# The order of SyncE's loads and stores ahead of the experts, in an attention layer with a mixture of experts

## The reference

```
xn = layernorm(x)
q, k, v = xn @ Wq.T, xn @ Wk.T, xn @ Wv.T      # 16 heads of 32; q and k get a rotary embedding
attn = softmax(causal(q @ k.T / sqrt(32))) @ v
gate_logits = xn @ gate_w.T                     # 8 experts
w = softmax(the two largest logits of a token)
y_all = xn @ expert_w.T + expert_b
out = x + attn @ Wo.T + sum over the two experts of w * y_all
```

## Time and profile before

| | |
|---|---|
| median of 3 runs | 1002.33 us (998.8 to 1003.36) |
| the profiled execution's own time | 999.5 us |
| its span, first to last instruction | 997.7 us |
| PE busy | 929.4 us (93%) |
| DVE busy | 742.8 us (74%) |
| POOL busy | 556.1 us (56%) |
| ACT busy | 435.7 us (44%) |
| granted TensorE clock, mean | 0.987 of full speed |
| 1 MB transfers, median from issue to landing | `x_in` 13.2, `w_in` 9.7, `xT_rows` 12.7, `w_rows` 7.9 us |

### The profile page before, as it was taken

The page is one execution under the profiler, slowest core; times in us unless marked ns, Lnnn a source line. Parts: engine busy times, 40 slices in busy tenths (PEclk is TensorE's granted clock), DMA queues, the critical chain, the costliest instruction groups (busy, mean ns, idle before and its releaser), DMA issues.

```text
span 997.7 us, 18754 instructions
## 1 busy us (share of the span) xinstructions
PE 929.4 (93%) x6589; PEld 447.2 (45%) x6589; DVE 742.8 (74%) x1327; ACT 435.7 (44%) x711; POOL 556.1 (56%) x553
## 2 busy tenths in 40 slices
PE   2899988989999999979999999989999999999887
PEld 1344444434444544435555555534444444444333
DVE  7988987887889899924444444477788888788865
ACT  5367866766766443331112111224434444334442
POOL 1545576674666556653333333247877888777641
PEclk9999999999999999999999999999999999999999
DMA  6366588698686353485555555454555564555431
GB/s 240 114 215 228 144 275 307 196 316 295 191 269 259 118 198 100 161 315 181 172 177 178 171 172 176 157 206 148 187 175 174 186 192 139 159 187 173 151 108 54
DMA packets 107963, 188.63 MB, mean 189 GB/s; under 512 B 11872, under 2 KB 65248, under 8 KB 102624
## 3 DMA queue, kind: packets, MB, share of 16 engines
q1 hardware_dynamic: 97072, 152.03, 44.2%
q0 software_dynamic: 10800, 35.40, 12.7%
HBM read 117.13 MB, written 70.25 MB: 188 GB/s over the span
## 4 chain that ended last, share of the span: by engine, by line
PE 67%; DVE 11%; POOL 9%; DMA 6%; ACT 3%; issue 2%; SPq 1%; DVEq 0%; ACTq 0%; POOLq 0%
PE psum L941 18%; PE psum L1026 10%; PE psum L1035 6%; PE psum L1050 6%; PE psum L989 6%; PE psum L976 5%; PE psum L958 5%; PE psum L992 5%; PE psum L918 4%; DMA x_in<-x 3%; DVE top L1476 3%; POOL gT L574 2%; PE psum L960 2%; POOL k_hl L583 1%; POOL pT L587 1%
## 5 line engine op out<-in xcount | busy, mean ns | idle before, releaser
L754 ACT ACTIVATE pT<-psum,factors 128x512 f32<-128x512 f32 (+1 forms) x352 | 219.5, 640 | 250.7 <-PE psum L976 241.3
L1476 DVE TENSOR_REDUCE top<-psum 128x1 f32<-128x384 f32 (+3 forms) x352 | 210.2, 634 | 22.7 <-PE psum L960 21.9
L1026 PE MATMUL psum<-xT,w_att 128*128 128x512 f16 x768 | 196.4, 381 | 6.6 <-DVE xT L1427 4.7
L941 PE MATMUL psum<-w_exp,x_gT 128*128 x852 | 197.7, 382 | 1.5 <-issue 1.5
L603 POOL DMA_INDIRECT x_g<-xn_rows,tok_of x71 | 67.4, 949 | 145.2 <-PE psum L918 137.2
L958 PE MATMUL psum<-k_stack,q_stack 96*128 96x384 f16 (+3 forms) x512 | 128.5, 304 | 17.4 <-DVE top L1476 16.5
L976 PE MATMUL psum<-q_stack,k_stack 98*128 98x256 f16 (+3 forms) x512 | 128.4, 304 | 5.8 <-ACT pT L754 4.5
L1432 DVE TENSOR_TENSOR x_gT<-psum,x_gT 128x512 f16<-128x512 f32 x71 | 49.0, 691 | 108.8 <-ACT x_gT L778 108.8
L941 PEld LDWEIGHTS psum<-w_exp,x_gT 128*128 128x128 f16 x852 | 84.0, 99 | 88.1 <-issue 4.5
L778 ACT ACTIVATE x_gT<-psum 128x512 f16<-128x512 f32 x71 | 42.3, 598 | 174.0 <-PE psum L918 174.0
L587 POOL TENSOR_SCALAR_AFFINE_SELECT pT<-pT 128x512 f32<-128x512 f32 x128 | 95.3, 754 | 18.4 <-ACT pT L754 18.2
(11 more groups left out here) (175 smaller groups left out, 1278.8 us busy)
## 6 DMA issues: line engine op xcount, KB each, us to landing
y_rows<-y_sb SPq DMA_DIRECT2D x71, 256.0 KB, 2.1
w_in<-w_all SPq DMA_DIRECT2D x12, 1024.0 KB, 9.7
q_stack<-qk_rows SPq DMA_DIRECT2D x96, 128.0 KB, 2.6
k_stack<-qk_rows SPq DMA_DIRECT2D x96, 128.0 KB, 2.6
x_in<-x SPq DMA_DIRECT2D x8, 1024.0 KB, 13.2
qk_rows<-q_hl SPq DMA_DIRECT2D x32, 256.0 KB, 2.1
qk_rows<-k_hl SPq DMA_DIRECT2D x32, 256.0 KB, 2.3
xn_rows<-x_in SPq DMA_DIRECT2D x8, 1024.0 KB, 4.8
```

What stands on the lines that cost most here:

```text
L754: act.activation(p_of(j, h, heads), banks[BANK_T + (NT_ * n + k) % 2][:, 0:W], ACT.Exp, scale=factors[:, 0:1]).then_inc(exp_done, 1)
L941: now = pe.matmul(banks[s % 4], x_gT[s % 4][:, xp * C + c, :], w_exp[:, bass.ds(e, 1), wp, c, :].rearrange("p e d -> p (e d)"), start=n == ...
L1026: now = pe.matmul(bank, w_att[:, what, wp, c, g * P:(g + 1) * P], xT[b % 2][:, xp * C + c, :], start=at_pass == 0, stop=at_pass == 3 * C - 1)
L1476: return dve.tensor_reduce(out=top[:, h:h + heads, i], in_=banks[BANK_S + k % 2][:, 0:heads * W].rearrange("p (h t) -> p h t", h=heads), a ...
```

## The change

Within a step's group of large transfers, the load of the next batch of x comes first, then the store of `gT`, and then the store of a pair and the load of the next matrix. What each waits for is the same as before, and no transfer is added or taken out.

```
@@ -474,14 +474,14 @@
                 if n in TAKE_AT:
                     take_xT(TAKE_AT[n])
+                if n in KEEP_AT:
+                    if KEEP_AT[n] + 2 < B:
+                        load_batch(KEEP_AT[n] + 2)
+                    store_gT(KEEP_AT[n])
                 if JOB_AT.get(n - 2, 0) >= NQ:
                     store_w(JOB_AT[n - 2])
                     if JOB_AT[n - 2] + 2 < NJ:
                         load_w(JOB_AT[n - 2] + 2)
-                if n in KEEP_AT:
-                    store_gT(KEEP_AT[n])
-                    if KEEP_AT[n] + 2 < B:
-                        load_batch(KEEP_AT[n] + 2)
```

## The result

| | before | after |
|---|---|---|
| median of 20 runs each | 1000.88 us (995.03 to 1004.83) | 1005.14 us (998.96 to 1009.26) |
| ratio, 95% interval | | 1.0042 [1.0027, 1.0057] |
| the profiled execution's own time, its span | 999.5, 997.7 us | 1000.18, 998.5 us |

The change makes the kernel slower by 0.42%, 4.2 us. The two profiled spans differ by 0.8 us only, so one pair of spans would have told the wrong story. The steps have to be read one by one. Both traces of the changed kernel are of quick executions, too (1000.18 and 1000.54 us, against a median of 1005.14): they place the loss, and what a median execution has beyond them is in no trace.

What follows compares the result with a forecast made beforehand. PE works 929.4 of 997.7 us, so SyncE's order can only move PE's idle time. Terms -1.1 + 2.6 + 1.5 + 0 + 2.2 = +5.2 us, from a mean of 1001.0, forecast 1006.2 us; range 1000 to 1012.

Steps and rivals of the forecast that it cites:

- A transfer takes the landing time of its place: SyncE's groups of large transfers: each lands when its new place in the order did before; one place is 2.4 us.
- The batch's waits go: DVE's statistics: the batch gains three places, 7.2 us, so the waits of 4.62 and 2.27 us both go.
- Step 4: DVE's wait of 4.62 us for a batch of x goes: -1.1 us, bounds -1.1 and 0.
- ACT's waits: ACT's high_w waits for the pair's store, by about 3.4, 5.5, 1 and 2.2 us in steps 3, 6, 9 and 10.
- Step 3: The pair lands at 144.0, ACT stands 3.4 us, 0.87 us of idle takes up part: +2.6 us, bounds 0 and 3.4.
- (c): Rival: stalls also slow PE's clock in steps 3 and 6, 1.2 us each; +8.4 us in all, 1009.4 us; chance 0.2.
- Step 6: ACT's high_w starts 4.8 us later, at 216.0; +1.5 us with the batch's 3.1 us gain included, bounds -3.1 and +4.8.
- The road by DVE: In step 6, low_w of 3.15 us starts behind high_w; PE's gates +1.0 us at full clock, +2.2 at the slow one.
- Step 9: The pair's store goes one place back, 2.4 us; ACT is 1.0 us short, its idle covers it: 0, bounds 0 and 1.0.
- Step 10: The pair takes the matrix's place, landing at 307.2; ACT wants it at 305.02: +2.2 us, bounds 0 and 2.2.
- (a): Rival: landings don't follow places, ACT barely waits, the batch comes early all the same; -4.2 us, 996.8 us; chance 0.08.
- (b): Rival: ACT's some 6 us of idle per step absorbs the stall, PE sees only half; +0.7 us, 1001.7 us; chance 0.27.

Runs made afterwards that it cites:

- by need: Against the kernel before, SyncE alone issues each step's group in the order its transfers are wanted, xT moved back where not urgent; ratio 0.9968 [0.9945, 0.9992].

## Why the prediction was right

The forecast was +5.2 us, 1006.2 us; measured were +4.2 us (2.7 to 5.7 by the interval) and 1005.14. Its mechanism is shown: the loss follows the place of the pair's store (none back 0.9975, one 0.9998, two 1.0042, three 1.0148) and sits in the steps where `high_w` waits for it. The sum is closer than its terms, which missed on both sides; that part is luck. I had also put what a measurement can tell at 5.0 us, and the 20 runs of each kernel told 4.2 us from nothing. Step by step:

- *A transfer takes the landing time of its place.* Right. The four landings of step 3 kept their times within 0.8 us. In step 6 they came 2.7 to 3.0 us later than their places (213.8, 216.5, 218.8, 221.9 against 211.1, 213.5, 216.0, 219.2), in a step that itself began 2.4 us later. Between 100 and 330 us of the eleven traces no 1 MB transfer whose landing they give overtook another.
- *The batch's waits go.* Right, all of them. Step 4: -1.1 us forecast, -0.5 and -1.1 in the two traces. In the first trace, where the gain was smaller, DVE waited 0.38 us for the blocks of a batch at 188.7 and ACT stood 1.51 us ahead of `copy_c`, 0.6 more than in the second. Why the blocks landed later was not settled.
- *ACT's waits.* Forecast 3.4, 5.5, about 1 and 2.2 us in steps 3, 6, 9 and 10; measured 4.74, 5.93, 0.41, 2.16, and 3.55, 6.06, 0.54, 0.44.
- *Step 3.* +2.6 forecast, +3.5 and +2.35 measured. In the first trace the wait was 1.3 us longer than worked out (ACT wanted the pair 0.5 us earlier than before, and it landed 0.8 us later than its place) and the clock fell behind it, which I had given to rival (c). (The piece of work from 150.97 to 153.86, which the prediction puts in step 4, is of this step.) The free 0.87 us held: 4.74 - 0.87 and 3.55 - 0.87 are 3.9 and 2.7 us, each 0.3 above what the step lost.
- *Step 6.* +1.5 forecast, +1.6 and +2.0 measured: the batch's wait and the pair's overlap, and one takes the place of the other. Without either the step takes 24.0 us, 2.9 less than before, where I had 3.1. But the two roads of my sum were not the ones that ended last, so that its +1.5 came out is luck in part. The road by DVE used a `low_w` of 3.15 us, which is that of step 10; the one of step 6 takes 2.30 (below), and the road gives 1.3 us at the slow clock in place of 2.2. And PE's 2.97 us for DVE was gone: it stood 3.96 us for ACT's exponentials, as in step 3, and did not wait for POOL at the gates.

```profile
214.61 2.30 DVE L1325 SCALAR_TENSOR_TENSOR w_hl<-w_in,up,w_hl 128x2048 f16<-128x2048 f32 x1
```

- *Step 9.* 0, and 0.
- *Step 10.* +2.2 forecast, +1.5 and 0.0. This is the term that was too large. In the first trace the wait was the 2.16 us forecast, but DVE's `low_w` behind it took 2.35 us in place of 3.15, which gave 0.8 back. In the second there was hardly a wait: the term rested on one landing (the matrix's, 13.0 us after its issue) which moves by nearly 2 us from one execution to the next.

Of the rivals, (a) is refuted. (b), ACT absorbs the stall, holds only for what I had counted as free, the 0.87 us before `copy_c`: in step 9 the wait of 0.4 to 0.5 us cost nothing. Of (c) the condition came true, and its price doesn't show: in step 3 the clock fell to 0.50 over a stretch where it had been 1.00, behind 3.65 us of standing and in the second trace behind 2.46, and yet the step lost 0.3 us less than the wait without its free 0.87 us. PE's 1.60 us of waiting for DVE is gone there, which took up at least a part of the slow matmuls' cost. In step 6 the clock was 0.94 before, 0.94 in the first trace and 0.88 in the second, where the step is 0.35 us longer than in the first. The sum of (c) was too high besides: it added 1.2 us for the slow clock in step 6 and then took the road that has these 1.2 us in it.

The remark on completion order from the Trainium skill, "DMA: Bandwidth & Descriptors", section "Queues, rings and completion order", changed nothing: it says what is not guaranteed, and this case shows the 1 MB transfers landing in the order of their issue. Within one of SyncE's groups they were mostly 2.4 us apart, at most 4.8. The prediction took the section for more of an objection than it is: it also says that the increment of the semaphore lands only after every earlier write of the same DMA engine. For transfers that are all split alike it does not let the pair land early.

## What to carry to other kernels

Before a transfer is moved forward in a busy queue, ask of every one that it passes who waits for it in the same step, stores included: a store that frees a buffer is as urgent as a load. With the queue full, a transfer's landing can be read off its place (here mostly 2.4 us for each 1 MB, but 4.8 us from the first to the second transfer of step 7), so the new waits can be worked out from the trace of the old kernel. And a single pair of spans can hide a change of 0.4%: compare the steps that the change touches, and find out which other stretches vary by themselves.

## What the hardware did that I had not expected

- A transfer issued by ACT left before work that stands ahead of it in ACT's program: issued at 193.10, 0.03 us after DVE had ended what it waited for, with the next of those activations starting at 193.29 and the last ending at 196.9. So the activations ahead did not hold it. That its semaphore alone does is not shown: in step 4 the transfer left at 150.38, 3.3 us after DVE had ended (147.08).
- Behind a standstill of 3.65 us PE ran at half clock for more than 4 us, in a step in which it had stood in pieces before without that (0.86 and 1.60 us, clock 1.00). The same two pieces do not always go without it: in the kernel "by need" the granted clock behind them was 0.62 over the stretch from 152 to 156 us.
- In step 1 to 2, which no kernel here changes, the length takes one of two values, 22.39 us (granted clock 0.92 in the trace of the kernel before) or 21.34 (1.00 in that of the kernel after).
